# A new slot table for the filler work of 64 attention steps

## The reference

```python
x = x + conv_attention(group_norm(x))      # 1x1 and strided 2x2 convolutions give Q, K, V; 4 heads of 32,
                                           # 1024 queries x 256 keys, softmax, layer norm, output projection
t = to_tokens(x)                           # 4 x 1024 tokens of 128
t = t + attention(layer_norm(t))           # one head of 64, 1024 x 1024, softmax, projection, + its input
h = layer_norm(t)
probs = softmax(h @ router.T); top 2 of 8 experts, renormalised
t = t + sum over the 2 experts of gate * (silu(h @ w1.T) * (h @ w3.T)) @ w2.T      # hidden 341
```

## Time and profile before

| | |
|---|---|
| median of 3 runs | 539.91 us (537.53 to 542.23) |
| profiled execution, span from first to last instruction | 536.8 us |
| prologue, 0 to 35.0 us | 35.0 us |
| the 64 steps, 35.0 to 330.6 us | 295.6 us |
| expert stage, 330.6 to 536.8 us | 206.2 us |
| busy over the span: PE, DVE, ACT, POOL | 86%, 63%, 55%, 34% |

### The profile page before, as it was taken

The page is one execution under the profiler, slowest core; times in us unless marked ns, Lnnn a source line. Parts: engine busy times, 40 slices in busy tenths (PEclk is TensorE's granted clock), DMA queues, the critical chain, the costliest instruction groups (busy, mean ns, idle before and its releaser), DMA issues.

```text
span 536.8 us, 11801 instructions
## 1 busy us (share of the span) xinstructions
PE 463.2 (86%) x3494; PEld 364.5 (68%) x3495; DVE 339.2 (63%) x1015; ACT 297.3 (55%) x782; POOL 182.4 (34%) x199
## 2 busy tenths in 40 slices
...
DMA packets 40059, 46.88 MB, mean 87 GB/s; under 512 B 6523, under 2 KB 29524, under 8 KB 40004
## 3 DMA queue, kind: packets, MB, share of 16 engines
...
q10 hardware_dynamic: 1162, 0.14, 0.2%
...
## 4 chain that ended last, share of the span: by engine, by line
PE 56%; DVE 17%; issue 10%; ACT 8%; DMA 6%; ACTq 1%; SPq 1%; POOL 1%; DVEq 0%; POOLq 0%
PE S L1434 12%; PE PO L1450 8%; PE S L1271 7%; PE TA L1442 3%; PE OM L1291 3%; ACT shared L711 3%; DVE lowest L902 3%; PE S L1257 3%; PE S L1258 2%; PE TA L1367 2%; DVE shared L911 2%; DMA xs<-slots 2%; PE OM L1285 1%; PE S L1253 1%; ACT shared L727 1%
## 5 line engine op out<-in xcount | busy, mean ns | idle before, releaser
L902 DVE TENSOR_REDUCE lowest<-S 128x4 f32<-128x1024 f32 (+1 forms) x64 | 78.0, 1219 | 56.5 <-PE S L1253 29.4
L1434 PE MATMUL S<-w_T,shared 128*128 x284 | 95.1, 457 | 3.9 <-ACT shared L809 3.0
L621 POOL DMA_INDIRECT y_rows<-shared,xs x71 | 68.3, 962 | 78.9 <-ACT shared L820 69.6
L1271 PE MATMUL S<-ident,shared 128*128 128x128 f32 x512 | 74.4, 286 | 6.4 <-ACT shared L711 4.0
L727 ACT ACTIVATE shared<-S 128x512 f32<-128x512 f32 (+1 forms) x64 | 51.9, 811 | 49.7 <-PE S L1271 49.6
L1183 DVE TENSOR_TENSOR late<-S,shared 128x341 f32<-128x341 f32 x71 | 36.4, 513 | 63.7 <-ACT shared L814 63.3
L814 ACT ACTIVATE shared<-S 128x341 f32<-128x341 f32 x71 | 32.4, 456 | 78.7 <-PE S L1434 77.6
L615 POOL DMA_INDIRECT slots<-rows_both,pos_i x64 | 62.4, 974 | 30.6 <-issue 17.8
L1271 PEld LDWEIGHTS S<-ident,shared 128*128 128x128 f32 x512 | 59.9, 146 | 16.7 <-ACT shared L711 9.1
L1450 PEld LDWEIGHTS PO<-w_T,shared 114*128 114x128 f32 x426 | 53.6, 193 | 23.4 <-issue 16.4
L1450 PE MATMUL PO<-w_T,shared 114*128 x426 | 61.4, 281 | 9.0 <-DVE shared L1188 5.6
...
## 6 DMA issues: line engine op xcount, KB each, us to landing
...
```

Of the source, the lines that this page charges most:

```text
L621: pool.indirect_dma_start(y_rows, bass.IndirectOffsetOnAxis(xs[:, k, C:C + 1].bitcast(I32), 0), ys[:, k % NC, :], None).then_inc(ys_out[k] ...
L902: nc.vector.tensor_reduce(lowest[:, g % 2, 0:n], S[g % 2][:, :].rearrange("p (h k) -> p h k", h=n), AX.X, ALU.min).then_inc(s["low_ready"], 1)
L1271: last = tr(S[g % 2][:, tile(k)], probs[:, g % 2, tile(k)], ident[:, :])
L1434: last = mm(S[k % 2][:, m * 512:m * 512 + H], xsT[:, k % NC, :], w13_T[:, bass.ds(e, 1), m * H:(m + 1) * H].rearrange("p a h -> p (a h)"), ...
```

## The change

The strings and their overlay are replaced by one written table of 192 slots (`SLOTS`), unit by unit; the loop over it is the same otherwise. The tables of the prologue (`FIRST`) and of the first 24 expert tiles (`LAST`) hold what they held. The one new unit, `ri`, is POOL's writing of row numbers, which stood ahead of all steps in POOL's queue (lines 611 and 612) and now stands in step 24. No arithmetic is added or taken away. Of the 207 units in the 64 steps 37 stay in their slot, 105 move by less than a step, 54 by one to three steps and 11 by more. These rows of the tables, old and new, are the ones used further down (`-` is an empty slot, and "to" shortens a run of units):

```diff
 step            slot 0            slot 1            slot 2
-conv 0,  0      wa.0              wa.1              wa.2
+conv 0,  0      wa.0+wa.1         wa.2 to wa.5      xn.1
-conv 0,  1      wa.3+xn.1         wa.4              wa.5+kT0.1
+conv 0,  1      wa.6+kT0.1        -                 qv0.1
-conv 0,  2      wa.6+kT1.1        wa.7+qv0.1        wb.0+qv1.1
+conv 0,  2      kT1.1             -                 wa.7+qv1.1
-conv 0,  3      wb.1+K.1          wb.2+Q0.1         wb.3+Q1.1
+conv 0,  3      wb.0+K.1          Q0.1+Q1.1         -
-conv 1,  8      xn.2              cs0.0             kT0.2          (xn.2 is now in step 7, slot 2)
-conv 1,  9      kT1.2             qv0.2+cs1.0       qv1.2
+conv 1,  9      kT0.2+kT1.2       cs1.0             qv0.2
+conv 1, 10      qv1.2             K.2               ca0.0
-conv 2, 16      l0.0              l1.0+cs0.1        m0.0
-conv 2, 17      m1.0              v0.0+cs1.1        v1.0
+conv 2, 16      l0.0+l1.0         -                 cs0.1
+conv 2, 17      wc.7+m0.0         cs1.1             -
+conv 2, 18      m1.0              ca0.1             v0.0+v1.0+ca1.1
+conv 2, 20      -                 -                 xn.3
-tok 0,  24      xn.3              cs0.2             kT0.3
-tok 0,  25      kT1.3             qv0.3+cs1.2       qv1.3
+tok 0,  24      -                 ts1.1+kT0.3       ri.0+ta0.1+ta1.1+qv0.3
+tok 0,  25      qv1.3             cs0.2+cs1.2       kT1.3
+tok 1,  42      cs1.3             -                 m1.2           (before: 41, slot 0; m0.2 40, slot 2)
+tok 2,  48      -                 ps0.1             m1.3           (before: 49, slot 0; m0.3 48, slot 2)
+tok 2,  49      ps1.1             -                 m0.3
-tok 2,  48-53   one unit x in each slot, x0.0 to xf.0
+tok 2,  52      x0.0 to xd.0      r0.1+r1.1+xe.0    pc.1
-tok 3,  58      pa0.2+x6.1        x7.1              x8.1+n3.1
-tok 3,  59      pa1.2+x9.1        r0.2+xa.1         r1.2+xb.1+n4.1
+tok 3,  57      x0.1 to x2.1, ps1.2, x3.1 to xe.1
+tok 3,  59      pa0.2+pa1.2+n3.1  n4.1+xf.1         r0.2+r1.2+g0.2+g1.2
```

The core of the code:

```diff
-AT = 1
-WEIGHTS = [[(u, e)] for u in ("wa", "wb", "wc") for e in range(E)]
...
-    ("conv", 0, overlay(WEIGHTS, (3, units(PRE, 1))), []),
-    ("conv", 1, overlay(units(PRE, 2), (AT, units(EARLY, 0))), []),
...
+SLOTS = table("""
+  wa.0+wa.1 wa.2+wa.3+wa.4+wa.5 xn.1
+  wa.6+kT0.1 - qv0.1
...
-            wait_copied(pool, ("wc", E - 2), ("wc", E - 1))
-            for k in range(2):
-                nc.gpsimd.iota(rows[k][:, :, C:C + 1].bitcast(I32), pattern=[[2 * P, 2 * NT]], base=k,
-                               channel_multiplier=2).then_inc(s["init_z"], 1)
...
+                elif u == "ri":
+
+                    wait_copied(pool, ("wc", E - 2), ("wc", E - 1))
```

125 lines of the change are left out of this document (81 added, 44 removed).

## The result

The changed kernel takes **516.95 us** (median of 4 runs, 515.63 to 519.43) against 539.47 us for the kernel before in the same comparison (4 runs). The ratio is 0.960, with a 95% interval of 0.956 to 0.964: 22.5 us or 4.0% less. Forecast were 532.0 us and a range of 520 to 544, so the direction was right and the size was about a third of what came.

A forecast was written before the change was run, and what follows sets the result against it. PE was taken as the bound: busy 266.4 of the steps' 295.6 us, idle 29. Terms -5.4 - 2.0 - 2.5 + 2.0 = -7.9 us, from 539.9 to 532.0 us; range 520 to 544.

The forecast's parts named there:

- Pixels and taps: Steps 1, 8, 24: ACT's copy no longer stands behind taps that wait for DVE's pixels; -5.4 us.
- the 1.4 that I put on such a stretch: Steps 24 and 25: estimated cost in us of one stretch at the 1.2 GHz clock, from 0.9 to 1.8.
- Queries and keys of the second attention: DVE's row minima wait less for ACT's part of m, four times; -2.5 us, bounds -7.0 and 0.
- Long units in slot 1: qv units of images 1 to 3 leave slot 1 for slot 2, ending ACT's idle time; -2.0 us, between -3.0 and 0.
- +1.0 for two `Q` in a slot: Step 3: Q0.1 and Q1.1 now share slot 1; +1.0 us, set against the -3.0 for qv.
- Three such places that come back for every image: Units holding up the ring behind them: xn at -5.4, qv at -2.0, m at -2.5 us.
- Piles: Several DVE units in one slot, largest in step 59, also steps 18 and 34; +2.0 us, between 0 and +8.
- Weights and sends: wa copies bunched in step 0 and POOL's sends bunched: no price, the copies 0 give or take 1.5 us.
- Clock: Low clock in conv 1 and tok 0: no change taken beyond the xn.3 stretch, 3.6 us either way.
- The rule that I cited: PE's throttled clock is the default and activity releases it; filling light steps wins 3.6 us, emptying steps loses as much.
- more than the sum: Rival, 14%: all lower bounds hold and the rest of the low clock goes too; 519 to 526 us.
- The rival of the ring: Rival, 26%: in conv steps, moved units carry their cost to a neighbour; -0.5, 539.4 us, case 535.5 to 543.

The follow-up runs named there:

- e2_qv: Old table with only the qv units of images 1 to 3 moved as in the new one: 543.04 us, ratio 1.004.
- e12_qvback: Changed kernel with qv0 and qv1 of images 1 to 3 back in slots 1 and 2 of one step: 518.59 us, ratio 0.964.
- e14_kq: Changed kernel with qv1, K, Q0 and Q1 of each of images 1 to 3 in one step again: 527.27 us, ratio 0.979.
- e4_three: Old table with only the pixel units xn, the qv units and l, m, v moved as in the new one: 532.49 us, ratio 0.987.
- e16_outback: Changed kernel with the output projections of images 0 and 1 (cs, ca, c, o, ts, ta) back in their old places: 523.22 us, ratio 0.968.
- e10_pre_early: e4_three plus the weight products of images 1 to 3 and the output projections of all four as in the new table: 520.75 us, ratio 0.967.
- e13_wold: Changed kernel with the transposes of the expert weights back at one a slot: 520.58 us, ratio 0.967.
- e8_pile: Changed kernel with DVE's pile of units in step 59 spread over steps 58 to 60: 518.14 us, ratio 0.962.
- e9_pre: e4_three plus the weight products (kT, qv, K, Q, V) of images 1 to 3 as in the new table: 529.01 us, ratio 0.982.
- e3_lmv: Old table with only the units l, m and v of the four images placed as in the new one: 535.46 us, ratio 0.992.
- e7_weights: e4_three plus the transposes of the expert weights as in the new table: 534.62 us, ratio 0.995.
- e18_spread: Changed kernel with its own fullest steps thinned (V.2, wc.7, ca1.1 and normalisations of image 1 moved to other steps): 518.18 us, ratio 0.962.

## Why the prediction was right in direction and too small

- **Pixels and taps (-5.4): right.** 4.9 us in the old table and 5.7 in the new one, each with one low stretch in it; the 1.4 that I put on such a stretch compares with 1.5 measured at 158.1 us.
- **Queries and keys of the second attention (`m`, -2.5): mis-sized**, within its bounds (-7.0 to 0). The old table gained 4.8, of which 2.3 through the clock; in the new one it is worth 6.1 in its own phases, all at full clock. I had charged the new places of `m` for putting the wait ahead of another instruction; DVE's wait of 8.4 us fell to 1.6, while the waits of its copies of probabilities for PE rose only from 2.8 to 4.2.
- **Long units in slot 1 (-2.0): the step failed in its reading.** By itself the move gives nothing (`e2_qv`: ratio 1.004, the phases 1.6 us longer). I priced the slot that `qv` leaves and not the step that `qv1` enters, where `K`, `Q0` and `Q1` already wait one behind another. In the new table `K` and `Q` move on as well, and only so does a part of the 2.0 appear (`e12_qvback`, some 1.3). For that I had one term, +1.0 for two `Q` in a slot. The move of `K` and `Q` is worth 8.2 us together with the place of `qv` (`e14_kq`), about 1 of it clock.
- **"Three such places that come back for every image": this is the step that failed.** The forecast priced nothing else as a gain, and the three gave 7.3 of the 23.9 us (`e4_three`). The list left out `K` and `Q`, and the output projections. Both could be read in the profile before: 6.6 us of DVE waiting for the halves of `Q`, and steps 12 and 20 of 7.0 (1.5 of it clock) and 5.5 us with `c1`, `o0`, `o1` in their three slots. The output projections of images 0 and 1 alone are worth 4.0 us (`e16_outback`), some 0.5 of it clock. The units of the routing and behind the second attention, with the sends, differ by 2.8 us between `e10_pre_early` and `e13_wold`; that pair is the only evidence for them, and which of those units it is was not tried.
- **Piles (+2.0): the sum was cut off too early.** Steps 58 and 59 did get 2.4 us longer, step 59 with 7.4 us near the 6.7 that I had summed. But the units piled there leave steps 60 and 61, which became 3.1 shorter, and these I did not count. Tok 3, which has the largest pile, got 1.0 us shorter, and spreading it gives 0.1.
- **Weights and sends (0, give or take 1.5): right** in the steps, at 0.9 and 0.3.
- **Clock (0): wrong.** The steps hold 16.0 us less at 1.2 GHz (20.6 to 4.6). The four stretches cost 4.0 us, and the 2.4 us less at the head of conv 0 some 0.5 by the price of `e8_pile`: an estimated 4.5 of the 23.9, which stand inside the other terms as well as beside them. The head begins ahead of the steps, so that part may be chance. The rule that I cited from the Trainium skill, "TensorE: Matmul & The Clock Gate", "What's actually happening", leaned to this side, and the trace agrees: PE idles less, and all phases but conv 0 are granted 1.00 now. I had set light steps against it (14, 15, 37 to 39); no stretch falls there after. Before, the one at 113.7 us did lie in steps 14 and 15, but what stands ahead of it is a wait of PE, as ahead of the other three; a step without units has PE busy for 3.19 of 3.51 us. It was waits that I had to count, and not steps with few units. How much each removed wait had to do with each stretch is not shown: the same tok 2 has a stretch in `e4_three` and `e9_pre` and none in `e3_lmv` and `e7_weights`.

The terms that undoing gives (5.7 + 8.2 + 4.0 + 6.8 + 0.9 + 2.8 = 28.4) are more than the 23.9 in all. Each undone part brings back a little of the clock, and parts in one step share a wait; the split is good to some 5 us, by the size of that excess. The rival "more than the sum" came nearest to the time (519 to 526), for another reason than the one written there: its bounds on `xn` and `m` nearly held, and the rest came from units not on the list. The rival of the ring is refuted for the table as a whole, which it had at 0.5 us less: units were moved to neighbours and most of the cost did not follow. For `qv` alone it held (`e2_qv`). Its opposite is refuted too: thinning does not always pay (`e18_spread`).
